# The projection job of an attention unit placed ahead of the unit's context matmuls, and its two readers moved with it

## What is computed

```python
q = _split_heads(query @ q_w.T + q_b, h) / scale
k = _split_heads(query @ k_w.T + k_b, h)
v = _split_heads(query @ v_w.T + v_b, h)
scores = jnp.einsum('bhqd,bhkd->bhqk', q, k)
attn = jax.nn.softmax(scores.astype(jnp.float32), axis=-1)
ctx = jnp.einsum('bhqk,bhkd->bhqd', attn, v)
out = ctx.transpose(0, 2, 1, 3).reshape(b, s, d) @ out_w.T + out_b
x = x + _layernorm(out)
```

## Time and profile before

| | |
|---|---|
| median of 3 runs (lowest, highest) | 2874.84 us (2865.7, 2875.46) |
| the profiled execution: time, span | 2873.4 us, 2871.6 us |
| busy, share of the span | PE 96%, DVE 78%, ACT 57%, POOL 33% |
| attention batch 3, from its first `pv` to that of batch 4 | 684.64 to 879.80 us |

### The profile page before, as it was taken

One profiled execution on the slowest core, in us unless ns is written; L12 is line 12 of the kernel. 1 busy time (PEld: TensorE's weight loads), 2 busy tenths in 40 slices (PEclk: granted clock), 3 DMA queues, 4 the chain that ended last, 5 costly groups with the idle time before them and its releaser, 6 DMA issues.

```text
span 2871.6 us, 47584 instructions
## 1 busy us (share of the span) xinstructions
PE 2760.4 (96%) x16514; PEld 1690.1 (59%) x16514; DVE 2241.4 (78%) x4679; ACT 1634.0 (57%) x3095; POOL 954.1 (33%) x997
## 2 busy tenths in 40 slices
PE   4999999999999999999998899999999999999997
PEld 2434333443343333433433378888888888888886
DVE  4898999999999989999999657666666666666664
ACT  1477777777777777777777743333333333333332
POOL 4041462543534634535335455111111111111112
PEclk8799999999999999999999999999999999999999
DMA  5213323343143234332332233222222222323221
GB/s 91 51 27 57 64 61 56 60 83 59 50 64 64 48 56 64 75 59 48 64 64 75 80 78 95 74 80 82 82 78 81 72 78 82 82 78 80 80 71 55
DMA packets 136639, 197.32 MB, mean 69 GB/s; under 512 B 22336, under 2 KB 84816, under 8 KB 134352
## 3 DMA queue, kind: packets, MB, share of 16 engines
q1 hardware_dynamic: 136400, 194.29, 30.7%
HBM read 108.74 MB, written 17.30 MB: 44 GB/s over the span
## 4 chain that ended last, share of the span: by engine, by line
PE 81%; DVE 6%; SPq 6%; ACT 3%; issue 2%; POOL 1%; DMA 1%; POOLq 0%; ACTq 0%; DVEq 0%
PE o_bank L544 14%; PE y_bank L667 13%; PE g_bank L653 13%; PE u_bank L653 13%; PE sm_bank L534 12%; PE st_bank L522 7%; DVE score_max L1017 4%; SPq L331 4%; PE job_bank L568 3%; ACT probs L906 2%; PE job_bank L577 2%; PE job_bank L589 1%; SPq L344 1%; SPq L356 1%; PE job_bank L608 1%
## 5 line engine op out<-in xcount | busy, mean ns | idle before, releaser
L1017 DVE TENSOR_REDUCE score_max<-sm_bank 128x1 f32<-128x512 f32 x2048 | 1300.8, 680 | 118.3 <-PE sm_bank L534 114.8
L906 ACT ACTIVATE probs<-st_bank 128x512 f32<-128x512 f32 x2048 | 1090.0, 600 | 340.3 <-PE st_bank L522 337.9
L534 PE MATMUL sm_bank<-qk_stack 64*128 64x512 f32 x2048 | 806.9, 466 | 28.0 <-DVE score_max L1017 14.0
L522 PE MATMUL st_bank<-qk_stack 64*128 64x512 f32 x2048 | 764.6, 456 | 31.0 <-ACT probs L906 26.9
L534 PEld LDWEIGHTS sm_bank<-qk_stack 64*128 64x128 f32 x2048 | 333.8, 188 | 594.9 <-DVE score_max L1017 548.8
L544 PE MATMUL o_bank<-probs,v_quad 128*32 128x512 f32 x4096 | 550.7, 610 | 6.5 <-ACT o_sb L814 6.5
L1174 DVE TENSOR_TENSOR h<-gate_act,u_bank 128x512 f32<-128x512 f32 x256 | 176.2, 688 | 314.4 <-ACT gate_act L868 314.4
L868 ACT ACTIVATE gate_act<-g_bank 128x512 f32<-128x512 f32 x272 | 162.4, 597 | 416.0 <-PE u_bank L653 415.9
L522 PEld LDWEIGHTS st_bank<-qk_stack 64*128 64x128 f32 x2048 | 318.7, 185 | 112.6 <-ACT probs L906 84.7
L879 ACT ACTIVATE h_hi<-h 128x512 fp32r<-128x512 f32 x272 | 172.1, 633 | 327.7 <-DVE h L1177 290.0
L667 PE MATMUL y_bank<-f_w_hi,h_hi 128*128 128x256 f32 x1088 | 311.8, 287 | 0.1
(11 more groups left out here) (197 smaller groups left out, 3857.5 us busy)
## 6 DMA issues: line engine op xcount, KB each, us to landing
cb<-comb_dram SPq DMA_DIRECT2D x256, 256.0 KB, 3.6
qk_stack<-qk_parts SPq DMA_DIRECT2D x360, 128.0 KB
x_in<-in_x SPq DMA_DIRECT2D x8, 1024.0 KB, 6.8
o_part<-o_sb SPq DMA_DIRECT2D x256, 32.0 KB, 2.0
sum_part<-o_sb SPq DMA_DIRECT2D x256, 32.0 KB, 2.0
x_res<-in_x SPq DMA_DIRECT2D x16, 512.0 KB, 3.9
x<-x_res SPq DMA_DIRECT2D x16, 512.0 KB, 3.1
f_x_in<-x SPq DMA_DIRECT2D x16, 512.0 KB, 3.9
```

Source lines behind the costliest of these rows:

```text
L522: mm(st_bank[tile % RING][:, :], k_stack[q][p][rows, kc * CH:(kc + 1) * CH], q_stack[q][p][rows, f * HALF:(f + 1) * HALF], start=True, sto ...
L534: mm(sm_bank[n % RING][:, :], q_stack[q][p][rows, tok:tok + CH], k_stack[q][p][rows, half * HALF:(half + 1) * HALF], start=True, stop=True ...
L906: nc.scalar.activation(probs[kc % 2][:, j, :], st_bank[(4 * U + j) % RING][:, :], ACT.Exp).then_inc(exp_done, 1)
L1017: v.reduce_max(score_max[f][:, HC * (2 * p + e) + c, half:half + 1], sm_bank[n % RING][:, :], AX_X).then_inc(smax_read, 1)
```

## The change

The job of a unit is issued behind `maximum(0, 0)`, directly ahead of `pv`, and no longer between `scores(3)` and `maximum(1, 1)`. ACT reads it one half unit earlier in its program, between the second and the third exponential of the next unit. DVE reads it in the unit of the job itself, between the first and the second reduction, and no longer at the start of the next unit. In the last batch, two small reads of the gate weights (`gT_lo`) move one unit ahead. Nothing is added to or taken from the work.

```diff
                     scores(0)
                     scores(1)
                     maximum(0, 0)
+                    if u in JOBS and not skipped(JOBS[u], first, last):
+                        kind, off, i, part = JOBS[u]
+                        job(kind, b + off, i, part)
                     if last and u == UNITS - 1:
                         gu(0, 0, 0, True)
                     pv(U, S, s, kc)
...
                     scores(2)
                     maximum(1, 0)
                     scores(3)
-                    if u in JOBS and not skipped(JOBS[u], first, last):
-                        kind, off, i, part = JOBS[u]
-                        job(kind, b + off, i, part)
                     maximum(1, 1)
...
                         nc.scalar.activation(probs[kc % 2][:, j, :], st_bank[(4 * U + j) % RING][:, :],
                                              ACT.Exp).then_inc(exp_done, 1)
+                        if j == 1 and u - 1 in JOBS and not skipped(JOBS[u - 1], first, last):
+                            kind, off, i, part = JOBS[u - 1]
+                            if kind in ("XT", "QK", "V", "OP") and part != 0:
+                                job(kind, b + off, i)
                     if kc == 0 and not (first and s == 0):
                         store_o(S)
-                    if u - 1 in JOBS and not skipped(JOBS[u - 1], first, last):
-                        kind, off, i, part = JOBS[u - 1]
-                        if kind in ("XT", "QK", "V", "OP") and part != 0:
-                            job(kind, b + off, i)
...
-                if u in (47, 49):
-                    gT_lo((u - 47) // 2)
+                if u in (46, 48):
+                    gT_lo((u - 46) // 2)
...
-                    if u - 1 in JOBS and not skipped(JOBS[u - 1], first, last):
-                        kind, off, i, part = JOBS[u - 1]
+                    if maxima:
+                        reduce(S + 2, (s + 2) % STEPS, kc, 0, (0,))
+                    if u in JOBS and not skipped(JOBS[u], first, last):
+                        kind, off, i, part = JOBS[u]
                         if part != 0:
                             job(kind, b + off, i)
                     if maxima:
-                        reduce(S + 2, (s + 2) % STEPS, kc, 0)
+                        reduce(S + 2, (s + 2) % STEPS, kc, 0, (1,))
```

More of the change, by code:

```diff
@@ L1008, in seed_a, with reduce @@
                 seed(seed_no(f"a{f}", B), var_a[f][:, :], mv_a[f][:, :, 1], rstd_a[f][:, :])
-            def reduce(S, s, kc, half):
+            def reduce(S, s, kc, half, es=(0, 1)):
                 f = s % 2
                 p, c = kc // HC, kc % HC
-                for e in range(2):
+                for e in es:
                     n = 32 * S + 4 * kc + 2 * half + e
```

## The result

The changed kernel takes 2972.41 us (median of four runs, 2969.41 to 2975.87) against 2872.16 for the kernel before (also four runs): a ratio of 1.0354, interval 1.0335 to 1.0373, slower. The forecast was 2958 with a range of 2930 to 2978. Its size was short by 14 us.

The account below looks back on a forecast made before the run. PE was taken to bound units with a job, which hides the fourth pair's wait for its readers. Terms 63 + 8 + 7 + 15 - 7 = 86 us on 2873.4 gave 2958 us, range 2930 to 2978.

Parts of the forecast that it names:

- The bound: Before, PE is gapless in units with a job; both unit kinds contain pv, first tile, reader, fourth tile, 2.28 us.
- The job, +0.28 in 224 units, +63 us: QK, V and OP units: the job behind the fourth pair no longer covers its wait, 3.51 us instead of 3.23.
- then takes its 0.33: In a job unit, the fourth pair, held until 2.28 us after pv, takes 0.33 us before the job's 0.90.
- The XT and SH terms: 28 units with XT jobs lose 0.28 us each, +8 us; 63 with SH jobs lose 0.11 each, +7 us.
- The turn of the fourth pair: Without a wait, the fourth pair would start 1.00 + 3 x 0.33 = 1.99 us after pv.
- Late reads, +15 us: At step starts, late job reads on DVE delay the first reduction and fourth pair, 2.1 us a batch; bounds 0 and 30.
- The gain, -7 us: DVE's read leaves crowded units without a job (25, 33, 57, 61), about 1 us a batch; bounds 0 and 21.
- (a): Job units stay at 3.23 us, the fourth pair not waiting or the stall made up; 2881 us; chance 4%.
- (b): Faster: DVE is the true bound and its reads move into idle time; 2852 to 2866 us; chance 3%.
- (c): Much slower: late reads carry over into several units; 2981 us, or 3000 if DVE falls behind in OP units; chance 9%.
- (d): PE's idling lowers the clock; at 1.2 GHz for a tenth of the attention stage, some +150 us; chance 1%.
- full in all but the first slices: Reading of the granted clock in the profile before the change, so that nothing in the forecast hangs on it.

Follow-up runs that it names:

- the first experiment: Against the kernel before, only PE's job moved directly ahead of pv, with ACT's and DVE's reads left in their old places: 3197.08 us in one run.

## Why the prediction was right, and where its size was off

**The bound.** Right. PE sets the units with a job before, and the chain of pv, first tile, its reader and the fourth tile sets them after. Its length of 2.28 us holds to 0.01, in the changed kernel and in the kernel that moves PE's job alone. The batches came out at 209.2 us, where about 206 was forecast and above 212 would have been wrong.

**The job, +0.28 in 224 units, +63 us.** The mechanism was right, the term too small: a V unit grew by 0.37 (3.23 to 3.60), a QK unit by 0.37 to 0.38. The step that failed is "then takes its 0.33". That was half the time of two pairs in a row, taken from the order before. The held pair needs 0.42 to 0.43 until the full-array matmul behind it. The number stood in the earlier trace rows: in the unit without a job the fourth maximum tile starts at 814.43 and the next pv at 814.85. The prediction put this end down to the exponentials alone. Both end there together: unit 61, without a job, lasts 2.70 in the changed kernel, 2.70 with halved exponentials, 2.70 with halved reductions, and 2.43 with both halved. With 0.09 more in each of 224, 28 and 63 units, 28 us were missing. The XT and SH terms were short by the same 0.09: without late reads an XT unit takes 3.29, not 3.20, and an SH unit 2.91, not 2.81.

The turn of the fourth pair was mis-sized as well, without harm to the sum, which goes by 2.28. In the changed kernel the first three pairs start 1.00, 1.33 and 1.56 us after pv, so the fourth would start at 1.80 and not at 1.99; it is held for 0.47. By the same pitches a job behind four pairs in one run would need 1.00 + 1.12 + 0.90 = 3.02 us if no ring held it, less than the 3.23 of the order before. That is an estimate from these rows; no kernel here reached it.

**Late reads, +15 us.** Too large. This is SH unit 24, whose XT read comes late, on PE:

```profile
799.84 1.07 PE L544 MATMUL o_bank<-probs,v_quad 128*32 128x512 f32 x8
...
802.05 0.50 PE L522 MATMUL st_bank<-qk_stack 64*128 64x512 f32 x1 [0.26 <-ACT probs L906]
802.53 0.50 PE L534 MATMUL sm_bank<-qk_stack 64*128 64x512 f32 x1
802.96 0.28 PE L581 MATMUL job_bank<-ident,row_max 128*16 128x128 f32 x1
```

The maximum tile starts 2.69 after pv and not 2.28, so the place and the way were right: 0.42 in unit 24, and 0.26 and 0.25 in units 32 and 56 (3.17 and 3.16 against 2.91), for which 0.56 was forecast. The unit ahead of 32 and of 56 is 3.60 long and not 3.51, and the one ahead of 24, an XT unit, 3.29; that the longer units give ACT and DVE time to get further fits this order, but no run tested it. Together with unit 22 (3.45) it is 1.1 us a batch, 8 in all, not 15.

**The gain, -7 us.** Right in place: units 57 and 61 went from 2.90 and 2.89 to 2.70 and 2.71, unit 25 from 2.91 to 2.70. It is larger in size. By difference, 12.1 + 1.5 + 1.7 + 1.1 of losses a batch (32 x 0.38, 4 x 0.38, 8 x 0.21 and the late reads) against 14.6 measured leaves 1.8 us a batch, about 12 in all. Units 10 and 18, after statistics, gained 0.2 each as well. Counted one by one, units 10, 18, 25, 28, 33, 57 and 61 give 1.4 of the 1.8. Another 0.3 is no gain of the change: in batches 1 and 3 of the profile before, unit 14 lasted 3.49 and 3.59 us instead of 2.7.

**The sum.** 86 us were forecast. 28 too little, 7 and 5 too much makes 102, as measured by the spans. The last term is itself the difference to the measured time, so the match is no test of it. That the time came out within the range is in part luck: with the job terms as measured and the other two as forecast the sum is 114 us, or 2987, above the 2978 of the range. Two errors the other way brought it back.

**The rivals.** (a) needed the fourth pair at its turn; it starts at 2.27, which the prediction named as the sign against it. (b) needed DVE's queue to set the end; DVE is idle 1.12 us in the V unit. The Trainium skill's advice to relieve the engine with the highest occupancy (Perfetto Trace Analysis, Identifying the Most-Contended Engine) gave 2866 in the prediction and would have been 106 us off. The kernel with half reductions shows that relief on DVE alone returns 0.06 us in a V unit. It returned 48 us in all, so DVE does cost time in this kernel; it does not set the loss by the job's place. (c) needed delays that carry over; the one unit with more than a late read, unit 4 at 3.96, had its 0.34 of backlog before too (3.05 against 2.70). (d) the clock stayed at 1.00 in batches 1 to 6 of the changed kernel. In the last batch it was 0.93, and 0.95 in the kernel before, about 7 us more at 1.2 GHz; at the rate of the first experiment that is 2 to 3 us of the 100. The prediction's "full in all but the first slices" missed this, because a 9 in the earlier trace rows only says 90% or more.

## What to carry to other kernels

With a ring of three banks and four tiles between two waits, the fourth tile is tied to the reader of the first; independent work of the in-order engine belongs **between** them. Here the job of 0.90 us adds 0.53 to a unit of 2.70 there, and behind the fourth tile all of its 0.90. Which of the places between is best depends on what else is held: two of three cost time. Before moving work past a wait, mark for each ring which tile is held and by which reader, and count the covers that the old place gave, on every ring. A read moved into an idle gap helps only if the tile it displaces isn't the one that the ring waits for, and a pitch read in one order must not be used for a piece that stands alone in the new one.

## What was not expected of the hardware

**A lone pair is dearer than a pair among pairs.** Two matmuls on different halves of the array, between full-array matmuls: one pair alone takes 0.44 us (866.11 to 866.55 in the kernel with the job behind the first pair), two in a row 0.66 (815.85 to 816.51), three 0.89 (828.69 to 829.58 in the kernel with the job behind the third). Each more costs 0.23, and a run as such 0.20. The first matmuls of a run have records of 0.49 to 0.50 us, those inside 0.39. That an unhidden load of the weights makes the difference fits these records and the waits put on PE's loads, but no run separated it; a cost of going over between half-array and full-array matmuls would fit as well. The Trainium skill (TensorE: Matmul & The Clock Gate, Architectural detail: the array is 16× 32×32, not 1× 128×128) has PE's queue pull weight loads ahead of running matmuls; a held pair, whose loads wait with it, would be the case where it can't. The trace of the changed kernel agrees as far as it goes: inside a run the record of a load starts ahead of its matmul (868.46 and 868.69), and that of the held tile together with it (869.57 and 869.57).

**The clock fell where PE idled more.** In the kernel with PE's part alone, the row of batch 3 from 810.69 to 1052.81 is

```profile
810.69:1052.81 242.12, 208.42 (x1193) 84.55 (x1193) 180.79 (x334) 149.20 (x289) 86.92 (x103) 0.93 0.27 49
```

PE is busy 208 of 242 us there, and the granted clock was 0.93 of the level of 2.4 GHz on average, by stretches at 1.2 GHz, 34 us in all. The third matmul of the job above, 0.6 us behind a hole of 1.36, took 0.55 us, against 0.39 to 0.40 elsewhere. In the changed kernel, with 194 of 209 us busy, the same batch had 1.00. In batch 3 the clock was 1.00 up to 894.77, where it fell for the first time, behind holes of 1.63 us (ahead of 888.82) and 1.29 us (ahead of 893.47). Rival (d) is a real mechanism, and the changed kernel stayed clear of it in batches 1 to 6.
